# Attention scores of a two-layer kernel: four square tiles of the array in place of two half-width tiles, and the softmax split by head

## The reference

```python
scores = jnp.einsum('bhsr,bhlr->bhsl', q_r, k_r)
attn = jax.nn.softmax(scores, axis=-1)
ctx_c = jnp.einsum('bhsl,bld->bhsd', attn, kv_rope)
ctx_lat = jnp.einsum('bhsd,hkd->bshk', ctx_c, w_kc_kv)
out = ctx_lat.reshape(b, s, H * K) @ Wo.T
```

## Time and profile before

| what | us |
|---|---|
| runs of the kernel: 3, median | 572.97 |
| lowest and highest of them | 570.17 and 573.07 |
| span of the profiled execution, first to last instruction | 573.3 |
| PE busy in it | 544.2 |
| DVE busy | 438.7 |
| ACT busy | 204.1 |
| POOL busy | 175.5 |

### The profile page before, as it was taken

One profiled execution on the slowest core, in us unless ns is written; L12 is line 12 of the kernel. 1 busy time (PEld: TensorE's weight loads), 2 busy tenths in 40 slices (PEclk: granted clock), 3 DMA queues, 4 the chain that ended last, 5 costly groups with the idle time before them and its releaser, 6 DMA issues.

```text
span 573.3 us, 10141 instructions
## 1 busy us (share of the span) xinstructions
PE 544.2 (95%) x3488; PEld 451.9 (79%) x3488; DVE 438.7 (77%) x932; ACT 204.1 (36%) x384; POOL 175.5 (31%) x153
## 2 busy tenths in 40 slices
PE   5599999999999999999998999999998999999995
PEld 4367666766676899878897888779987888888885
DVE  6979888988897657896785776786579876776676
ACT  3224132313234403333324555653142443443331
POOL 3914101110140002655400212220043654564550
PEclk9899999999999899999999999989999999999999
DMA  8202220122023000011110443010000111111102
GB/s 270 90 1 73 74 74 0 73 73 88 40 71 127 1 2 0 3 55 55 55 50 10 134 142 94 1 56 1 2 1 27 31 53 55 41 41 55 55 0 73
DMA packets 12778, 30.80 MB, mean 54 GB/s; under 512 B 2512, under 2 KB 4944, under 8 KB 12752
## 3 DMA queue, kind: packets, MB, share of 16 engines
q1 hardware_dynamic: 12752, 30.46, 16.5%
HBM read 29.40 MB, written 1.05 MB: 53 GB/s over the span
## 4 chain that ended last, share of the span: by engine, by line
PE 68%; issue 14%; DVE 12%; POOL 3%; DMA 1%; ACT 0%; SPq 0%; DVEq 0%; POOLq 0%
PE ps L404 17%; PE ps L406 17%; PE ps L405 17%; PE ps L556 7%; POOL probs L332 2%; PE ps L452 2%; PE ps L504 2%; DVE X L1266 2%; PE ps L462 1%; DMA W<-attn 1%; PE ps L711 1%; PE ps L425 1%; DVE newton L1032 1%; PE ps L433 1%; DVE probs L1083 1%
## 5 line engine op out<-in xcount | busy, mean ns | idle before, releaser
L359 POOL TENSOR_TENSOR PT_lo<-qc,PT_hi 128x512 fp32r<-128x512 f32 x48 | 62.5, 1304 | 89.8 <-ACT PT_hi L762 89.8
L1266 DVE SCALAR_TENSOR_TENSOR X<-ps,coef,X 128x256 f32<-128x256 f32 x200 | 81.1, 475 | 0.1
L332 POOL TENSOR_TENSOR probs<-probs,rowrec 128x512 f32<-128x512 f32 x28 | 28.6, 1043 | 169.6 <-DVE rowrec L1093 169.3
L404 PE MATMUL ps<-xs_hi,WG_hi 128*128 128x512 f32 x200 | 79.5, 398 | 0.9 <-DVE qc L1282 0.9
L406 PE MATMUL ps<-xs_hi,WG_lo 128*128 128x512 f32 x200 | 79.1, 396 | 0.0
L405 PE MATMUL ps<-xs_lo,WG_hi 128*128 128x512 f32 x200 | 79.0, 395 | 0.0
L1277 DVE SCALAR_TENSOR_TENSOR qc<-qc,ps 128x512 f32<-128x512 f32 x50 | 34.3, 686 | 46.0 <-PE ps L406 45.6
L404 PE MATMUL ps<-WD_hi,PT_hi 128*128 128x256 f32 x200 | 57.5, 287 | 4.8 <-DVE X L1266 3.0
L405 PE MATMUL ps<-WD_lo,PT_hi 128*128 128x256 f32 x200 | 56.6, 283 | 0.0
L406 PE MATMUL ps<-WD_hi,PT_lo 128*128 128x256 f32 x200 | 56.5, 283 | 0.0
L762 ACT ACTIVATE PT_hi<-ps 128x512 fp32r<-128x512 f32 (+1 forms) x64 | 35.7, 601 | 58.1 <-PE ps L462 52.8
(11 more groups left out here) (123 smaller groups left out, 1214.3 us busy)
## 6 DMA issues: line engine op xcount, KB each, us to landing
WF<-ffn SPq DMA_DIRECT2D x25, 384.0 KB, 3.0
W<-attn SPq DMA_DIRECT2D x8, 704.0 KB, 4.2
W<-attn SPq DMA_DIRECT2D x8, 672.0 KB, 4.2
W<-attn SPq DMA_DIRECT2D x16, 320.0 KB, 4.4
X<-x SPq DMA_DIRECT2D x4, 256.0 KB, 5.1
out<-X SPq DMA_DIRECT2D x8, 128.0 KB, 1.8
probs<-kvT SPq DMA_DIRECT2D x1, 512.0 KB, 6.1
G<-kvTrot SPq DMA_DIRECT2D x1, 512.0 KB, 6.3
```

The lines of the kernel that those rows point to most:

```text
L332: nc.gpsimd.tensor_tensor(part, part, rowrec[:, 4 * h:4 * h + 4, :].unsqueeze(3).to_broadcast([P, 4, 2, L]), ALU.mult).then_inc(s.p, 1)
L359: nc.gpsimd.tensor_tensor(hT[u][1][:, h * HALF:(h + 1) * HALF], hid[:, pair, :], hT[u][0][:, h * HALF:(h + 1) * HALF].bitcast(F32), ALU.su ...
L404: nc.tensor.matmul(dst, lhs[0], rhs[0], start=start, stop=False)
L1266: V.scalar_tensor_tensor(X[:, t, :], psum[4 + t // 2][:, (t % 2) * DM:(t % 2 + 1) * DM], coef[:, t, bass.ds(i, 1)], X[:, t, :], ALU.mult, ...
```

## The change

The keys are stored once for each head's partitions (`keys`, 128 x 16 x 64), with no zeros. Each product of the scores contracts 64 partitions (one head), has 64 stationary columns and streams 64 columns: four square tiles of the array, by head (rows) and batch (columns). Head 0 goes to PSUM bank 6, head 1 to bank 7. In front of each half stands a product with one column over all 128 rows (`ident`), which carries the wait for `G`. There is one signal `s.s` for a round, after all 32 products, in place of one for each half. The halves of the softmax are now the heads: DVE waits for the whole round, and PE's transposes wait for both heads. The clearing of `kbd` goes, and its two copies become one.

```diff
-        kbd = sb("kbd", [P, NB, 2 * L])
+        keys = sb("keys", [P, NB, L])
...
-            nc.gpsimd.memset(kbd[:], 0.0).then_inc(zeros_ready, 1)
...
-                        part = probs[:, 4 * h:4 * h + 4]
+                        part = probs[:, :, h]
                         nc.gpsimd.tensor_tensor(
-                            part, part, rowrec[:, 4 * h:4 * h + 4, :].unsqueeze(3).to_broadcast([P, 4, 2, L]),
+                            part, part, rowrec[:, h].unsqueeze(2).to_broadcast([P, NT, L]),
                             ALU.mult).then_inc(s.p, 1)
...
             def scores(s, i):
+
                 for h in range(2):
                     pe.wait_ge(s.g_ev, 2 * i + h + 1)
-                    for t in range(4):
+
+                    nc.tensor.matmul(psum[6][0:S, 4 * h * L:4 * h * L + 1], ident[:, 0:S], ident[:, 0:1], start=True,
+                                     stop=True)
+                    for t in range(4 * h, 4 * h + 4):
                         for b in range(2):
-                            tok = (4 * h + t) * P + b * S
-                            last = nc.tensor.matmul(psum[6 + h][b * S:(b + 1) * S, t * P:(t + 1) * P],
-                                                    G[:, tok:tok + S], kbd[:, 2 * (4 * h + t) + b, :],
-                                                    start=True, stop=True)
-                    last.then_inc(s.s, 1)
+                            tok = t * P + b * S
+                            for a in range(2):
+                                head = slice(a * DC, (a + 1) * DC)
+                                last = nc.tensor.matmul(psum[6 + a][b * S:(b + 1) * S, t * L:(t + 1) * L],
+                                                        G[head, tok:tok + S], keys[head, 2 * t + b, :],
+                                                        start=True, stop=True)
+                last.then_inc(s.s, 1)
 
             def transposes(s, i, banks):
 
+                pe.wait_ge(s.p, 2 * i + 2)
                 for h in range(2):
-                    pe.wait_ge(s.p, 2 * i + h + 1)
                     for t in range(4):
...
-                copy(kbd[0:DC, :, 0:L], kvT_s[0:DC])
-                copy(kbd[DC:P, :, L:2 * L], kvT_s[DC:P]).then_inc(kbd_ready, 1)
+                copy(keys[:], kvT_s).then_inc(keys_ready, 1)
...
             def softmax_shift(s, i):
 
+                dve.wait_ge(s.s, i + 1)
                 for h in range(2):
-                    dve.wait_ge(s.s, 2 * i + h + 1)
-                    sc = psum[6 + h][:].rearrange("p (t a l) -> p t a l", t=4, a=2)
-                    mx = rowmax[:, 4 * h:4 * h + 4, :]
+                    sc = psum[6 + h][:].rearrange("p (t l) -> p t l", l=L)
+                    mx = rowmax[:, h]
                     V.tensor_reduce(mx, sc, AX, ALU.max).then_inc(s.max, 1)
                     dve.wait_ge(s.max, 2 * i + h + 1)
-                    V.tensor_tensor(probs[:, 4 * h:4 * h + 4], sc, mx.unsqueeze(3).to_broadcast([P, 4, 2, L]),
+                    V.tensor_tensor(probs[:, :, h], sc, mx.unsqueeze(2).to_broadcast([P, NT, L]),
                                     ALU.subtract).then_inc(s.sub, 1)
```

More of the change, by code:

```diff
@@ L110, in build @@
         probs = sb("probs", [P, NT, 2, L])
-        rowmax = sb("rowmax", [P, NT, 2])
-        rowsum = sb("rowsum", [P, NT, 2])
-        rowrec = sb("rowrec", [P, NT, 2])
+        rowmax = sb("rowmax", [P, 2, NT])
+        rowsum = sb("rowsum", [P, 2, NT])
+        rowrec = sb("rowrec", [P, 2, NT])
         PT = split("PT", [P, HP, TOK])
@@ L143, in build @@
         COLS_READY, ROWS_READY = 3, 3 + 4 + 2 + 2
-        kbd_ready, vbd_hi, kv_ready = sem("kbd_ready"), sem("vbd_hi"), sem("kv_ready")
+        keys_ready, vbd_hi, kv_ready = sem("keys_ready"), sem("vbd_hi"), sem("kv_ready")
         out_written = sem("out_written")
@@ L314, in vbd_lower @@
             def vbd_lower():
-                pool.wait_ge(zeros_ready, 4)
+                pool.wait_ge(zeros_ready, 3)
                 pool.wait_ge(vbd_hi, 1)
@@ L561, in body @@
                     if first:
-                        pe.wait_ge(kbd_ready, 1)
+                        pe.wait_ge(keys_ready, 1)
                     else:
@@ L857, in attention0 @@
                 transposed_tiles(0, 1, (6, 7))
-                act.wait_ge(zeros_ready, 3)
+                act.wait_ge(zeros_ready, 2)
                 act.wait_ge(context_step, COLS_READY)
-                copy(kbd[0:DC, :, 0:L], kvT_s[0:DC])
-                copy(kbd[DC:P, :, L:2 * L], kvT_s[DC:P]).then_inc(kbd_ready, 1)
+                copy(keys[:], kvT_s).then_inc(keys_ready, 1)
                 body(0, first=True)
@@ L1088, in softmax_sums @@
                 for h in range(2):
-                    part, rec = probs[:, 4 * h:4 * h + 4], rowrec[:, 4 * h:4 * h + 4, :]
+                    part, rec = probs[:, :, h], rowrec[:, h]
                     dve.wait_ge(s.exp, 2 * i + h + 1)
-                    V.tensor_reduce(rowsum[:, 4 * h:4 * h + 4, :], part, AX, ALU.add).then_inc(s.sum, 1)
+                    V.tensor_reduce(rowsum[:, h], part, AX, ALU.add).then_inc(s.sum, 1)
                     dve.wait_ge(s.sum, 2 * i + h + 1)
-                    V.reciprocal(rec, rowsum[:, 4 * h:4 * h + 4, :]).then_inc(s.rec, 1)
+                    V.reciprocal(rec, rowsum[:, h]).then_inc(s.rec, 1)
                     if normalise:
                         dve.wait_ge(s.rec, 2 * i + h + 1)
-                        V.tensor_tensor(part, part, rec.unsqueeze(3).to_broadcast([P, 4, 2, L]),
+                        V.tensor_tensor(part, part, rec.unsqueeze(2).to_broadcast([P, NT, L]),
                                         ALU.mult).then_inc(s.p, 1)
@@ L1340, in _ @@
             dve.wait_ge(gate_ready, 1)
-            dve.wait_ge(zeros_ready, 4)
+            dve.wait_ge(zeros_ready, 3)
             layer_norm(1, lambda t: add_output(at[0], 0, t), (0, 1), lower_at=NT - 1)
```

## The result

The changed kernel is slower: 590.67 us (median of 4 runs, 589.26 to 591.21) against 571.57 for the kernel before (4 runs, 569.89 to 573.07), ratio 1.0324 with a 95% interval of 1.028 to 1.0368. The forecast was 586, the range 577 to 602.

A forecast was written before the change was run, and what follows sets the result against it. The prediction took the softmax round trip over PE, DVE, ACT and POOL as the bound, not PE's busy time; 2.3 (first attention) + 6.9 (second) + 3.9 (ends) = 13.1 us on 572.97 gave 586 us, range 577 to 602.

The forecast's parts named there:

- The bound: Both attentions: the softmax round trip over PE, DVE, ACT and POOL sets the rounds; slack 0.41 us in the first.
- What the array gains: Score products: four square tiles run abreast, 0.055 us for four, so 0.44 a half in place of 0.88.
- The second rival: Score products: squares do not run four abreast; two at a time 601 us, one at a time 630; chance 17%.
- What the half pays: Each half of the scores: one-column product 0.11, tiling change 0.20, squares 0.44, sum 0.75 us; another 0.20 between halves.
- cheap squares: Scores: one-column products and tiling changes hide, leaving the wait for both heads, 5.5 us, so 578.5; chance 17%.
- The rounds: Rounds grow 0.27 us in the first attention, 0.96 in the second; with the last rounds 2.3 and 6.9 us.
- The ends: Ends of both attentions: later start and lost overlap with the second half's normalising cost 2.0 and 1.9, sum 3.9 us.
- the sum: Whole kernel: first attention 2.3, second attention 6.9 and the two ends 3.9 make 13.1 us.
- The clock: Second attention: PE idle 1 us before transposes lowers the clock, 1.7 us in each of 7 rounds, 598; chance 15%.
- Faster, PE as the bound: Rounds of both attentions: they shrink by what PE saves, 11.9 us, to 561; chance 6%.
- Cost nothing: Clearing of `kbd` on POOL, one key copy (1.05 us) on ACT and the softmax's strided slices change no time.

The follow-up runs named there:

- e1: Kernel before with one score signal a round, after both halves, in place of one for each half; half-width tiles kept: 583.38 us, ratio 1.021.
- e3: Kernel before with both the single late signal and the transposes' wait for both halves, without the squares: 594.43 us, ratio 1.0395.
- e4: Changed kernel without the one-column products, PE's loops of rounds written out: 584.05 us, ratio 1.021.
- e2: Kernel before with PE's transposes waiting for both halves of the softmax: 579.38 us, ratio 1.012.
- e5: Changed kernel with products that nobody reads (fillers) where PE idles at the two ends: 584.38 us, ratio 1.0205.
- e7: Kernel before with fillers, products nobody reads, in its own idle stretches at the two ends: 569.07 us, ratio 0.9949.
- e11: Kernel before with fillers at the ends (e7) and PE's two loops of rounds written out: 569.87 us, ratio 0.999.
- e9: Squares with softmax by token halves and fillers (e8), without one-column products, PE's loops written out, against the kernel before: 564.90 us, ratio 0.9886.
- e6: Square tiles with the softmax split by token tiles and a signal for each half, against the kernel before: 570.80 us, ratio 0.997.
- e10: Changed kernel with PE's two loops of rounds written out and nothing else: 589.80 us, ratio 1.0326.
- e8: Squares with the softmax by token halves (e6) plus e7's fillers at the ends, against the kernel before: 570.17 us, ratio 0.9966.

## Why the prediction was right, and where it was short

**The bound.** Right. The loop over DVE had 0.41 us of slack in the first attention, and DVE's start moved from S+1.09 to 1.83 behind the round's first instruction: 0.74 - 0.41 = 0.33, which is what the round grew by. In the second attention there was 0.17 as long as each half had its own wait: in e1 DVE's start moves by 2.01 - 1.21 = 0.80 and the round by 0.63. Behind the wait for both heads there was none: e3's round grows by 0.80 + 0.26.

**What the array gains.** Right: four squares abreast at 0.0575 us, taken at 0.055. The second rival (two at a time, or one) is out. The Trainium skill, "TensorEngine Tiling (Array Packing)", section "Performance Considerations", puts some 60 cycles of overhead on a product; at 2.4 GHz that is an estimate of 0.025 us a record. e4's 64 records start and load in 1.02 us, 0.016 each, and the measurement decides.

**What the half pays.** Right in kind, a little dear. From one half's squares to the next, 338.72 - 337.89 = 0.83 where 0.95 was put down; the signal came at 1.80 from the round's first instruction, not 1.91. e4 shows what the changes of tiling and the one-column products cost in the end, 0.57 a round. So *cheap squares*, the first rival, is out too.

**The rounds.** 9.41 - 8.56 = 0.85 where 0.96 was forecast, for the same reason; 0.33 where 0.27 was, since DVE started 0.06 later than worked out (1.83 against 1.77). e1 and e2 show the two parts by themselves in the second attention, 0.63 and 0.25; together, in e3, they make 1.06, more than their sum, since in e1 the first half of the transposes still went ahead on its own signal (PE's transposes start 0.94 us ahead of POOL's end there).

**The ends: the step that was mis-sized.** "Sum 3.9" for the two ends measured 2.20 + 4.30 = 6.5 in the traces, and the last round of the second attention, put at 1.1, measured 2.0. The lost overlap itself was priced right: the first end came to 2.20 against 2.0; with the clock held (e5) that last round costs 8.57 - 7.53 = 1.04, and the second end 201.77 - 200.05 = 1.7 with as long a stretch at 1.2 GHz as before, against 1.9 in the sum. What was left out is the clock behind PE's idle stretches in that last round and at the second end: 13.6 us at 1.2 GHz, where the kernel before has 3.4. Holding it gave back 0.97 + 2.58 = 3.55 in the traces; the ends and that round together measured 8.5, 3.5 over the 5.0 that was put down for them. At the first end both traces have 6.8 us, and it cancels there. *The clock*, the third rival, saw the mechanism and put it in the wrong place: it forecast 1.7 us in each of 7 rounds, for gaps of 1 us; in six of them the clock stayed at 1.00, and only the seventh, idle for 2.27, had a stretch at 1.2 GHz behind it. Its price in the medians is less sure: without fillers on either side the change costs 3.24 points, with fillers on both 2.56 by e7 and 2.15 by e11, so 0.7 to 1.1 points, 4 to 6 us, are the clock's.

**Faster, PE as the bound.** Out: DVE's start moved later in both attentions, by 0.74 and 0.59 from the round's first instruction, against the earlier trace rows. What the rival counted on is there, though: with an early signal again (e9) PE's shorter scores do shorten the rounds, by 0.40 and 0.25.

**Cost nothing.** The clearing of `kbd` and the copy are not seen: scores start 0.25 earlier in the trace after, but the traces differ by more than that at this place (37.95 in e6, 42.57 in e2). DVE's maxima take 0.68 to 0.69 as before, ACT's exponentials 0.63 and POOL's two multiplications 2.04 as before, so the slices by head cost nothing there.

Still open: e3 lies 6 us above what was expected of it, and the changed kernel's medians lie as far above the sum (19.1 - 13.1 = 6.0), at the same mean granted clock (0.969 to 0.975 in e3's six runs, 0.972 to 0.975 in the changed kernel's four). e3's trace has stretches of 10.2 us at 1.2 GHz at both ends, but no filled version of it was run. What makes such a stretch long, short or absent isn't settled: e1's trace has none at the first end, and there the changed kernel, with PE idle for 2.12 us, has the same 6.8 as the kernel before with 0.74. The kernel before was profiled in one of its longer executions, 3.5 above the median. No shorter one was traced, but of its runs beside e9 to e11 nine with a mean granted clock of 0.989 or above took 566.5 to 570.8, seven at 0.983 to 0.988 took 570.3 to 574.7.

## What to carry to other kernels

Look at which dimension a new tiling splits the work along: when each consumer needs both parts, two halves that were pipelined become one barrier, and a loop that is a round trip over four engines pays for it in each turn, however fast the array has become. Here the same squares with the halves left by token tiles, and with no product between them that changes the tiling (and with fillers at the ends, which gave the kernel before 0.1 to 0.5%), beat both kernels by 1% and 4%. An array gain inside such a loop shows only as long as the results reach their consumers no later than before, so that PE does not come to wait for the round trip.

When a change leaves TensorE idle at the end of a stage, read the granted clock of the next microseconds before pricing the gap: here a gap of 2.3 us had 6.8 us at half the clock behind it, and holding the clock from there to the end of the attention gave back 3.5 us, while gaps of 0.9 to 1.0 us inside the rounds cost no clock.

## What the runs showed that was not expected

- A loop body of two alternating rounds ran 18.92 and 19.05 to 19.13 us in e6; written out (and without the one-column products, e9) the rounds are 18.65. Writing out alone made 19.11 into 19.05 (e11) and 19.43 into 19.37 (e10).
- The stretches at 1.2 GHz differ from trace to trace at the same place: 6.8 us at the first end before, none in e1, 10.2 in e3; none (e6) to 10.2 us (e3) at the second. So sums over rounds met the traces closely, while three totals (e2, e3, e8) missed what was expected by more than their rounds did.
- PE idle for 0.86 to 1.03 us ahead of the transposes in each of six rounds left the granted clock at full speed in those rounds.
- A control took back a small gain: the fillers' 0.5% on the kernel before (e7, interval wholly below 1) was not there in e11.
